# State space stage of an eight-layer kernel: one convolution product per scan step instead of two, and the output product cut into four pieces

## The reference, cut to what matters

```python
xz = x @ W_in
xc, z = jnp.split(xz, 2, axis=-1)                 # 256 channels each
xp = jnp.pad(xc, ((0, 0), (D_CONV - 1, 0), (0, 0)))
xconv = conv_b
for k in range(D_CONV):                           # 4 taps
    xconv = xconv + xp[:, k:k + Ll, :] * conv_w[:, k]
xs = jax.nn.silu(xconv)
x_dbl = xs @ W_x                                  # d_raw, Bp, Cp
delta = jax.nn.softplus(d_raw * w_dt + b_dt)
def step(h, inp):
    dt, b, c, xt = inp
    At = jnp.exp(dt[..., None] * A)
    h = At * h + (dt * xt)[..., None] * b[:, None, :]
    y = jnp.einsum('bdn,bn->bd', h, c)
    return (h, y)
_, ys = jax.lax.scan(step, h0, seq)
y = (jnp.swapaxes(ys, 0, 1) + xs * D) * jax.nn.silu(z)
return y @ W_out
```

## Time and profile before

| | |
|---|---|
| median of three executions | 2899.3 us (2894.75 to 2900.53) |
| the profiled execution, its own time | 2890.57 us |
| its span, first to last instruction | 2888.8 us |
| PE / DVE / ACT / POOL busy, share of the span | 77% / 68% / 53% / 42% |
| granted PE clock, mean | 0.877 of full |
| state space stage | about 1436 to 2074 us of the span |
| in the stage | DVE 543.9 us busy of 638, PE 460.9 |

### The profile page before, as it was taken

How to read it: one execution, slowest core, us unless ns; L and a number is a source line. 1 busy time by engine, 2 the same in 40 slices (tenths; PEclk the granted TensorE clock), 3 DMA queues, 4 the chain that set the end, 5 groups by cost and what they waited for, 6 DMA issues and landing times. The chain is left out here.

```text
span 2888.8 us, 48994 instructions
## 1 busy us (share of the span) xinstructions
PE 2211.7 (77%) x17390; PEld 1126.7 (39%) x17406; DVE 1965.7 (68%) x3727; ACT 1533.0 (53%) x3059; POOL 1210.7 (42%) x1267
## 2 busy tenths in 40 slices
PE   6999988886899895664847777777523876889886
PEld 2333324554444443553713333333223872323232
DVE  7888857665657563663278888888762227888884
ACT  4788872122556563331456666666321224767775
POOL 5423203332434311442456666666573434532310
PEclk9999997787999997776959999998856997999998
DMA  3121220000112112104830000000014971222110
GB/s 118 25 45 28 41 66 1 1 1 1 38 38 46 35 32 61 24 24 139 273 93 0 0 0 1 1 0 1 0 41 153 291 239 39 36 45 55 37 31 16
DMA packets 127626, 152.81 MB, mean 53 GB/s; under 512 B 19992, under 2 KB 108760, under 8 KB 126776
## 3 DMA queue, kind: packets, MB, share of 16 engines
q1 hardware_dynamic: 120792, 136.12, 17.6%
q0 software_dynamic: 6592, 13.56, 1.3%
HBM read 96.15 MB, written 25.59 MB: 42 GB/s over the span
## 5 line engine op out<-in xcount | busy, mean ns | idle before, releaser
L479 DVE TENSOR_REDUCE a_mx<-banks 128x2 f32<-128x1024 f32 (+3 forms) x768 | 805.9, 1087 | 234.3 <-PE banks L1051 128.3
L892 ACT ACTIVATE a_prob<-banks 128x512 f32<-128x512 f32 (+3 forms) x1536 | 744.7, 541 | 268.7 <-PE banks L1089 146.6
L1116 PE MATMUL banks<-a_prob,a_vaug 128*32 128x256 f32 (+2 forms) x5632 | 432.0, 388 | 0.2
L2236 POOL TENSOR_TENSOR m_hc<-m_h,m_cs 128x512 f32<-128x512 f32 x256 | 332.4, 1320 | 139.3 <-DVE m_h L2090 138.7
L1089 PE MATMUL banks<-a_Qs,a_Ks 64*128 64x512 bf16 (+3 forms) x1536 | 325.2, 364 | 48.2 <-DMA a_Qs<-a_negm 25.3
L1042 PE MATMUL banks<-a_Ks,a_Qs 63*128 63x512 bf16 (+3 forms) x1536 | 285.0, 368 | 37.2 <-DVE a_mx L479 30.4
L2090 DVE TENSOR_TENSOR_SCAN m_h<-banks,m_u 128x512 f32<-128x512 f32 x256 | 300.8, 1207 | 15.8 <-issue 13.7
L2386 PE MATMUL banks<-m_hc,kc 128*128 128x512 f32 x512 | 292.8, 656 | 9.6 <-DVE m_yf L2218 8.5
L2293 ACT ACTIVATE banks<-m_dt,acoef 128x512 f32<-128x512 f32 x256 | 174.3, 688 | 115.8 <-DVE m_h L2090 114.6
L1042 PEld LDWEIGHTS banks<-a_Ks,a_Qs 63*128 63x128 bf16 x1536 | 74.2, 93 | 329.7 <-issue 163.7
L1116 PEld LDWEIGHTS banks<-a_prob,a_vaug 128*32 128x32 f32 x5632 | 118.8, 109 | 155.8 <-issue 115.4
(11 more groups left out here) (437 smaller groups left out, 4167.4 us busy)
## 6 DMA issues: line engine op xcount, KB each, us to landing
c_wbuf<-in_w2e SPq DMA_DIRECT2D x71, 512.0 KB, 4.3
b_wbuf<-in_w1e SPq DMA_DIRECT2D x39, 578.0 KB, 4.5
a_Ks<-a_parts SPq DMA_DIRECT2D x252, 64.0 KB
a_Qs<-a_parts SPq DMA_DIRECT2D x252, 64.0 KB
rows_in<-in_unused SPq DMA_DIRECT2D x1, 4579.5 KB, 17.7
c_yb<-rows_in SPq DMA_DIRECT2D x71, 64.5 KB, 4.5
a_mixed_in<-rows_back SPq DMA_DIRECT2D x16, 256.0 KB, 4.3
a_Qs<-a_negm SPq DMA_DIRECT2D x192, 2.0 KB
```

Source lines behind the costliest of these rows:

```text
L479: dve.tensor_reduce(both[:, :, c], m_bank(u)[:, :, 0:keys[c % NT]], AX.X, ALU.max).then_inc(S("m_read"), 1)
L892: act.activation(prob[:, n % DEEP, first_query[kt]:T], s_bank(u)[:, first_query[kt]:T], ACT.Exp, scale=scale).then_inc(S("s_read"), 1)
L1116: i = pe.matmul(V[32 * hl:32 * hl + 32, q0:q1], vaug[:, b % 3, kt, g % NG * GH + hl, :], prob[:, (4 * a + hl) % DEEP, q0:q1], start=kt == ...
L2236: gp.tensor_tensor(hc[:, n % 6, :], h[:, n % 4, :], cs[:, k % 4, :], ALU.mult).then_inc(S("weighed"), 1)
```

## The change

Only due times change, and with them the order in the lists. The convolution products are due one in each step over eight steps (T + 4.6, 8.6, ... 32.6), where before two stood in each of four steps. What follows them is moved: the xs activation on ACT from T + 23.2 to T + 34.0, the B/C projection on PE from T + 33.0 to T + 36.6, the step-size projection from T + 35.0 to T + 38.6. The gate products, due at T + 53.0 and T + 54.9, are now due at T + 52.6 and T + 56.6. The output product, all at T + 9.0 before, is cut by its four blocks of 128 positions and due at T + 9, 11, 13 and 15; the final add on DVE moves from T + 13.0 to T + 16.6.

```diff
@@ vector_batch
-                    yield end + 13.0
+                    yield end + 16.6
                     dve.wait_ge(S("out_projected"), b + 1)
@@ scalar_batch
-                    yield t + 29.2
+                    yield t + 40.0
                     for c in range(NCH):
                         act.wait_ge(S("in_projected"), 4 * b + c + 1)
@@ tensor_batch
-                        yield t + 10.6 + 4.0 * (n // 2) + 2.4 * (n % 2)
+                        yield t + 10.6 + 4.0 * n
...
-                    yield t + 39.0
+                    yield t + 42.6
                     pe.wait_ge(S("silu"), 4 * b + 2)
...
-                    yield t + 41.0
+                    yield t + 44.6
...
-                        yield t + 59.0 + 1.9 * c
+                        yield t + 58.6 + 4.0 * c
                         pe.wait_ge(*((S("rest"), b + 1), (S("pos_ready"), b + 1))[c])
...
                     for j in range(NT):
+                        if j:
+                            yield at(DS * (b + 1)) + 9.0 + 2.0 * j
                         for c in range(NCH):
```

## The result

The changed kernel takes 2926.2 us (2919.6 to 2932.4), the kernel before 2897.7 in the same comparison: a ratio of 1.010, interval 1.0084 to 1.0116. Forecast was 2926, which is 2899.3 + 27; measured is 2897.7 + 28.5. A second comparison gave 1.0111 (1.0084 to 1.0139).

The account below looks back on a forecast made before the run. DVE's scans were taken to set the pace, 71.67 us a batch. The terms summed to +35 us at half clock, +11 at full; +27 was taken, 2926 on the median, likeliest range 2915 to 2937, 8 in 10 within 2907 to 2940.

Parts of the forecast that it names:

- the discount: Over the whole sum: two thirds of the way from full clock (+11 us) to half clock (+35) taken, giving +27.
- Part 1: One convolution product per step: waits of `u` for PE shrink, -1.6 us in first scanned batch, -0.25 in next six.
- Part 2: Output product cut in quarters: final add waits for the fourth, +1.0 us in each of six batches, +1.1 in last.
- Part 3: Xs activation between step 9's decays delays a scan and the projections: +2.3 us a batch at half clock, +0.6 at full.
- Its rival with 5.7 us of slow clock each time: At the projections, one more slow pass pair, 7 x 1.1 us: +42, 2941; chance 0.06.
- Part 4: Second gate product behind next batch's first B spread delays last scan: +2.1 us at half clock, +0.4 at full, seven times.
- the wait of `u` 11: In the kernel before, `u` 11 waits 1.80 us, put down to four projection products in one step on PE.
- The rival that the relief of PE's backlog would be kept: Only PE's backlog held DVE; waits of `u` and final add go, 26 us: 2873; chance 0.10.
- The rival that the clock stays up: PE keeps full clock after the longer idle stretches: +11 us, 2910; chance 0.10.
- The +5: Part 3's price if the skill page's table-switch drain held, making the xs activation block some 2.8 us longer.

Follow-up runs that it names:

- rebalanced kernel: Kernel before with final add at T + 16.6 and convolution products at T + 4.6, 6.0, 8.6, 12.6, 16.6, 19.0, 20.6, 23.0; ratio 0.9953.

## Why the prediction was right

The mechanism was right: each new stall came at the place and from the cause that the prediction gives. That the number fits to a fraction of a microsecond is luck in part: the terms of the sum (-3.1, +7.1, and with the discount +12.1 and +10.8) were off by up to 5 us each, in opposite directions, the trace has 30.8 for 27, and the runs of one kernel spread over 6 us (before) and 13 us (changed). In the trace of after, per term:

- **Part 1, convolution**: -1.6 and -0.25 in six batches, -3.1. The wait of `u` in those steps is gone. Right.
- **Part 2, output product**: the wait was 2.29 in six batches (forecast 2.4, was 1.31), right to a tenth, and +1.0 a batch with it. The last batch was wrong: the add waited 1.19 instead of a forecast of 3.5, since PE wasn't at half clock there this time (0.97 from 2045 to 2062, against 0.50 in the earlier trace rows); in the second profile it waited 2.26. Term -1.2 instead of +1.1; part 2 as a whole 4.6 instead of 7.1. Its cause is shown by the kernel with the product in one piece.
- **Part 3, xs activation and projections**: waits of 14.2 (seven scans of 2.03), 23.1 (`rest`) and 14.4 (the polynomial's first step; the other 1.19 each are as before), against 12.3, 12.5 (`u` 11) and 9.7: +17.2, or 2.5 a batch. The price at half clock was 2.3, 16.1 for seven batches, and with the discount 12.1. The step that was off is the discount of a third: in the first profile all seven batches ran this at half clock, and three of them for longer than 3.4 us (`rest` waited 3.94 to 3.99 there and 2.75 to 2.88 in the other four). In the second profile one of the seven had full clock there, and `rest` waited 1.34 in it. Its rival with 5.7 us of slow clock each time was true of those three.
- **Part 4, gate products**: the last-scan waits are 13.4 instead of 3.4 (13.2, and 0.15 at another scan), and 2.1 more behind them (yf 1.5, `u` 0.6, which I had put at nothing): +12.1, between the ends of 2.8 and 14.7 and near the two thirds taken (10.8). In three batches the gate product ran at full clock (1.02 us, and a wait of 0.8), in the others not (1.54 to 1.92 us, and 2.33 to 2.36, once 3.74).

Sum: -3.1 + 4.6 + 17.2 + 12.1 = 30.8, the stage's growth.

What I had wrong without its changing the number: that the wait of `u` 11 was PE's four projection products. It was 0.6 of that and 1.2 of half clock; the change removed both there and put 3.3 at `rest`. The rival that the relief of PE's backlog would be kept is out: with the convolution and the projections alone the ratio is 1.0033. The rival that the clock stays up is out for part 3, and holds for three of the seven batches in part 4.

Of the drain of 1380 ns that the Trainium skill (ScalarE: Activation LUTs, What ACT_TABLE_LOAD costs) has for a table switch nothing shows after the change either: 1694.23 to 1698.10 is 3.87 us for two loads and two activations. The +5 that the prediction worked out from it doesn't follow in any case: a block longer wherever it stood would have held up the kernel before as well.

What stays open is where the half-clock stretches fall in a given run; the differences of a few us between versions that change only this can't be forecast from one trace.

## What to carry to other kernels

Spreading one engine's work evenly helps only the engine that waits for it; ask for each piece that is moved which chain it was moved into. Here a block of 3.9 us on ACT, put between two halves of a step instead of between steps, held the row copy that releases PE's next spread, and moving it out was worth 21.5 us of the stage, part of it by the clock. A product cut into pieces among other work ends later than one in a piece, and its consumer waits for the last piece. And where PE's clock falls, an idle stretch is paid for twice: by the wait and by the slow work behind it, here 1.35 us of the wait of `rest` against 2.75 to 3.99.

## What the runs showed of the hardware that had not been expected

After an idle stretch of the same length PE's clock isn't always at half, and the slow stretch doesn't always start with the work. In the rebalanced kernel the same B spread after the same 2.52 us of idle time was followed by full clock in one batch, and in another by a slow stretch that began only after the spread and one 32-bit product (the last two rows are at half clock, a 32-bit product of 1.91 us instead of 1.02 and a spread of 0.63 instead of 0.39):

```profile
1738.03 0.39 PE L2361 MATMUL banks<-m_G,kb 96*128 96x512 bf16 x1 [2.52 <-ACT m_cs L2283]
1738.26 1.02 PE L2386 MATMUL banks<-m_hc,kc 128*128 128x512 f32 x2
...
1875.53 0.39 PE L2361 MATMUL banks<-m_G,kb 96*128 96x512 bf16 x1 [2.52 <-ACT m_cs L2283]
...
1876.95 1.91 PE L2386 MATMUL banks<-m_hc,kc 128*128 128x512 f32 x2
1878.65 0.63 PE L2361 MATMUL banks<-m_G,kb 96*128 96x512 bf16 x1
```

The granted clock of the 3.4 us from the first of these restarts is 1.00, of those from the second 0.68.

In the kernel before each batch took 71.67 us and lost its clock at the same places each time, and so did the changed kernel with the output product in one piece, at 75.1 us a batch. In the changed kernel itself, with batches of 74.9 to 77.6 us, the places alternate from batch to batch: `rest` waits 3.94, 2.75, 3.99, 2.77 and so on. Extra spreads in PE's idle time kept full clock behind them: in the changed kernel both projections then took 1.88 us and the stage was 7.5 us shorter, in the rebalanced one `u` 11 waited 0.6 in every batch and the stage was 5.6 us shorter.
